# Two transformer layers on one core: the four compute engines' instruction orders laid out anew

## The chip, the core and the metric

The kernel runs on one core of one Trainium2 chip. Its time is the device time of one execution in microseconds (us); less is better. A core has four compute engines that each work through an instruction list of their own in the order in which it was written: TensorE (PE in the profile), VectorE (DVE), ScalarE (ACT) and GpSimd (POOL). SyncE (SP) issues nearly all DMAs here, also in written order. Engines wait for each other through semaphores only. An instruction that waits holds up everything that is behind it on its engine.

## The reference

Input is one sequence of 2048 tokens with 128 features. Four blocks follow, each `x = x + block(layernorm(x))`:

```python
x = x + L0_attn(layernorm(x))   # 16 heads of 64: softmax over the own segment of 64 and over
                                # positions at distance 4, 8, ..., 256; then w_o
x = x + L0_ffn(layernorm(x))    # blockwise FP4 quantised gate, up and down products, silu
x = x + L1_attn(layernorm(x))   # RMS norms, gated linear recurrence in chunks of 64, an MLP of 512
x = x + L1_ffn(layernorm(x))    # token shift, sigmoid gate, squared relu
```

The first block is the attention, with projections q, k and v of 1024 columns. The other three work token by token, but for the recurrence and the token shift.

## The kernel before, in words

The attention is cut into 32 units, numbered 0 to 31: 8 pairs of heads times 4 windows of 512 tokens. Unit U has pair U // 4 and window U % 4. Each unit passes through these steps, which are small functions in the code, called with the unit and often with a part:

- on PE: `project(U, 1)` and `project(U, 0)` make keys and queries (lines 403 to 405), `scores(U, 0)` and `scores(U, 1)` the two halves of the scores (line 422), `turn(U, 0..3)` transposes four parts of the weights (line 464), `weigh(U, 0..3)` multiplies them by the values (lines 484, 495, 498), and `output(U)` by w_o (line 510). For the values themselves there are 32 calls `values(i)` (lines 388 to 390), all before the loop.
- on DVE: `seg_max` (lines 731, 733), `band_max` (line 719), `seg_sums` (741), `differences` (750, 754), `factors` (761 to 771), `even_turned` (780), which copies the transposed parts 0 and 2 out of PSUM, `accumulate` (792), and `take_values` of odd index (836).
- on ACT: `take_keys`, `take_queries` (601, 609), `band_exps`, `seg_exps` (569, 577), `exp_difference` (616), `odd_turned` (585) for parts 1 and 3, `take_out` (593), and `take_values` of even index (644).
- on POOL: `keys_by_class`, `queries_by_class` (930, 938), `scale_band`, `scale_seg` (948, 957).

The softmax has two halves, which lie differently over the partitions. Each unit therefore sends its maxima and sums to DRAM and reads them back in the other layout: `send_statistics` (lines 306, 307) and `fetch_statistics` (314, 315) on SP. `differences` of the unit waits for the landing of that. `factors` and the scaling on POOL follow, and the turns wait for the scaling.

A list written out by hand sets the order of units 0 to 3 with all `values`; SP stores each of these values (line 268) between the exchanges. Then a loop `for t in range(6, 33)` has one iteration on each engine for a step. In iteration t PE projects unit t, makes the scores of unit t-2 and turns and weighs units t-5 and t-6. After the loop a second list finishes the attention and interleaves it with the token blocks of layers 0 and 1. These go in four groups of 512 tokens (g = 0 to 3), with steps such as `t1`, `x1`, `bn0`, `qx0`, `z0`, `rs0` (lines 1100 and on). Group g begins with `t1(g)`, which needs `accumulate(28 + g)`.

PSUM has eight banks. Scores take banks 0 to 3. Banks 4 and 5 hold the turned parts, even parts in 4 and odd in 5, and before the loop the values of even and odd index. Each of the two holds one such part at a time, so a turn waits for the copy of the part before. `weigh` fills bank 6. Bank 7 is shared by keys, output and queries in turn; the list `occupants` says in which order. Statistics, `pband` and `pseg` have four slots, rows of keys and queries three.

Of the kernel before, what the change touches and what calls it, by code (L numbers as in the profile page):

```python
# [22 lines left out]
P = 128  # L23
# [85 lines left out]
def attention(nc, ctx, hidden, w_q, w_k, w_v, w_o, w_gate, w_up, w_down, plain_weights, columns, ident, constants,  # L109
# [121 lines left out]
    occupants = [(0, "key")]  # L231
    for x in range(1, FIRST_STEP):
        occupants += [(x, "key"), (x - 1, "query")]
    occupants.append((FIRST_STEP - 1, "query"))
    for t in range(FIRST_STEP, NS_ALL + 8):
        occupants += [(t - lag, who) for who, lag in (("key", 0), ("wo", 7), ("query", 0)) if there(t - lag)]
# [21 lines left out]
    with nc.Block() as block:  # L258
# [106 lines left out]
        def _(pe):  # L365
# [148 lines left out]
            keep_busy(7); turn_rows(0); keep_busy(4)  # L514
            values(0); values(1); values(2); project(0, 1); turn_rows(1); values(3); project(1, 1); values(4)
            values(5); turn_rows(2); values(6); project(0, 0); values(7); values(8); project(2, 1); values(9)
            values(10); turn_rows(3); scores(0, 0); scores(0, 1); values(11); values(12); project(1, 0); values(13)
            values(14); project(3, 1); values(15); scores(1, 0); scores(1, 1); project(2, 0); values(16); values(17)
            project(4, 1); values(18); values(19); scores(2, 0); scores(2, 1); values(20); values(21); project(3, 0)
            values(22); values(23); values(24); project(5, 1); values(25); values(26); scores(3, 0); values(27)  # L520
            values(28); project(4, 0); values(29); values(30); project(5, 0); values(31); turn(0, 0); scores(3, 1)
            turn(0, 1); turn(0, 2)

            for t in range(FIRST_STEP, DRAIN):
                project(t, 1)
                weigh(t - 6, 0)
                weigh(t - 6, 1)
                turn(t - 6, 3)  # L530
                output(t - 7)
                turn(t - 5, 0)
                weigh(t - 6, 2)
                scores(t - 2, 0)
                weigh(t - 6, 3)
                scores(t - 2, 1)
                project(t, 0)
                turn(t - 5, 1)
                turn(t - 5, 2)
# [3 lines left out]
            output(26); turn(27, 3); weigh(27, 0); weigh(27, 1); weigh(27, 2); scores(31, 0); weigh(27, 3)  # L543
            scores(31, 1); turn(28, 0); turn(28, 1); output(27); turn(28, 2); turn(28, 3); weigh(28, 0); weigh(28, 1)
            weigh(28, 2); weigh(28, 3); turn_weights(0); turn_weights(1); turn(29, 0); output(28); turn_weights(2)
            turn(29, 2); turn(29, 1); t1(0); turn_weights(3); turn_weights(4); turn(29, 3); turn_weights(5)
            weigh(29, 0); weigh(29, 1); weigh(29, 2); weigh(29, 3); turn_weights(6); turn(30, 0); turn(30, 1)
            output(29); turn_weights(7); turn(30, 3); turn(30, 2); weigh(30, 0); weigh(30, 1); t1(1); weigh(30, 2)
            weigh(30, 3); turn(31, 1); t2(0); turn(31, 0); turn(31, 3); output(30); turn(31, 2); gu0(0); t1(2)
            weigh(31, 0); weigh(31, 1); weigh(31, 2); weigh(31, 3); gu1(0); output(31); t2(1); t1(3); gu2(0); gu0(1)  # L550
            gu3(0); gu1(1); t2(2); gu2(1); gu0(2); gu1(2); t2(3); gu3(1); gu0(3); gu2(2); t3a(0); gu1(3); t3b(0)
            gu3(2); dn(0); gu2(3); t3a(1); t3b(1); gu3(3); dn(1); t4(0); pv(0); pk(0); t3a(2); pg(0); t3b(2); pa(0)
            pq(0); t4(1); dn(2); qq(0); pv(1); t3a(3); pk(1); t3b(3); pg(1); dn(3); pa(1); t4(2); pq(1); trx(0)
            qq(1); pv(2); pk(2); pg(2); t4(3); op(0); pv(3); trx(1); pq(2); pk(3); pa(2); pg(3); pa(3); op(1); qq(2)
            pq(3); t5(0); qq(3); trx(2); fc1(0); fc0(0); trx(3); fc3(0); t5(1); fc2(0); fc0(1); fc1(1); op(2); pr(0)
            fc2(1); fc3(1); op(3); t5(2); pr(1); fc0(2); fc1(2); t5(3); fc2(2); fc3(2); fc1(3); fc0(3); t6(0); fc3(3)
            pr(2); t6(1); fc2(3); k(0); pr(3); r(0); t6(2); k(1); k(2); kv(0); t6(3); r(1); kv(1); r(2); k(3); kv(2)
            r(3); kv(3)

        @block.scalar  # L560
        def _(act):
# [93 lines left out]
            split_v(0); deviations(0); split_qk(0, 1); take_hi(0); split_qk(0, 0); take_values(0); deviations(1)  # L655
            take_keys(0); take_hi(1); take_values(2); deviations(2); take_keys(1); take_values(4); take_hi(2)
            deviations(3); take_values(6); split_v(1); take_queries(0); take_values(8); take_keys(2); take_values(10)
            take_hi(3); band_exps(0, 0); take_values(12); take_queries(1); take_values(14); take_keys(3); seg_exps(0)
            band_exps(0, 1); take_queries(2); take_values(16); seg_exps(1); band_exps(1, 0); take_values(18)
            take_keys(4); band_exps(1, 1); take_values(20); seg_exps(2); take_values(22); take_queries(3)  # L660
            take_values(24); band_exps(2, 0); exp_difference(0); take_keys(5); take_values(26); band_exps(2, 1)
            take_values(28); take_queries(4); take_values(30); band_exps(3, 0); exp_difference(1); take_queries(5)
            odd_turned(0, 1); take_keys(6); seg_exps(3); odd_turned(0, 3); band_exps(3, 1)
            for t in range(FIRST_STEP, DRAIN):
                exp_difference(t - 4)
                take_out(t - 6)
                take_queries(t)
                odd_turned(t - 5, 1)
                take_keys(t + 1)
                band_exps(t - 2, 0)  # L670
                odd_turned(t - 5, 3)
                seg_exps(t - 2)
                band_exps(t - 2, 1)
                if t in (6, 7):
                    split_qk(1, 7 - t)
                if t in (QUANT_STEP + 2, QUANT_STEP + 7, QUANT_STEP + 12):
                    coarse_weights((t - QUANT_STEP) // 5)

# [3 lines left out]
            exp_difference(29); take_out(27); band_exps(31, 0); odd_turned(28, 1); odd_turned(28, 3); seg_exps(31)  # L682
            band_exps(31, 1); take_out(28); exp_difference(30); take_weights(0); take_weights(1); take_weights(2)
            odd_turned(29, 1); take_weights(3); odd_turned(29, 3); take_weights(4); z0(0); take_out(29)
            exp_difference(31); odd_turned(30, 1); take_weights(5); take_weights(6); take_weights(7); qx6(0)
# [12 lines left out]
        def _(dve):  # L698
# [139 lines left out]
            def blocks(x):  # L838
                return x.rearrange("p (b x) -> p b x", x=QB)
# [82 lines left out]
        def _(pool):  # L922
# [74 lines left out]
            for t in range(FIRST_STEP, DRAIN):  # L997
# [5 lines left out]
                if t == 8:  # L1003
                    tail_constants(pool, constants, s_made, s_cols)
# [983 lines left out]
```

## Time and profile before

| | us |
|---|---|
| three runs | 470.03, 474.9, 470.95 |
| median | 470.95 |
| span of the profiled execution, first to last instruction | 468.2 |
| PE busy | 443.3 (95%) |
| DVE busy | 394.1 (84%) |
| ACT busy | 333.0 (71%) |
| POOL busy | 296.5 (63%) |

The profiled execution has no total time beside its span. The fastest of the three runs is 1.8 us over that span, the median 2.75 us. A matmul's end is modelled in the profile, and matmuls overlap, so a PE that is called busy in all of a stretch has had no gap of its own there; it says nothing on how much work was in it.

### The profile page before, as it was taken

The numbers are of one execution on the slowest core, as the hardware profiler recorded it, in microseconds if no ns is written. First come the engines' busy times: TensorE is split into PE (matmuls) and PEld (weight loads), VectorE is DVE, ScalarE is ACT, GpSimd is POOL, SyncE is SP. The second block draws the span as 40 slices with busy tenths as digits, with TensorE's granted clock in tenths as the row PEclk, the third lists the DMA queues.
The fourth block names the chain that finished last, engine by engine and source line by source line (L and its number), as shares of the span: only waits on it lengthen the run. The fifth ranks groups of instructions, "written<-read, shape, count | busy, mean of one in ns | idle before, by whom it ended". The sixth has DMA issues, their size and how long they took to land.

```text
span 468.2 us, 17264 instructions
## 1 busy us (share of the span) xinstructions
PE 443.3 (95%) x6440; PEld 348.8 (74%) x6440; DVE 394.1 (84%) x1344; ACT 333.0 (71%) x975; POOL 296.5 (63%) x491
## 2 busy tenths in 40 slices
PE   7999699999999999999999899998987989999996
PEld 5687588888888888888787678887744757558775
DVE  5888598997988899799797697996899989998775
ACT  3678668778768777877786678695566579987533
POOL 4222576687576768667865587665669897674322
PEclk9999999999999999999999999999999999999999
DMA  6477952356345335445455564464000000000003
GB/s 224 175 254 201 276 122 53 75 115 123 75 84 110 74 74 109 81 78 109 86 116 122 110 135 90 77 123 91 1 1 0 0 2 0 2 0 2 1 0 91
DMA packets 136098, 40.53 MB, mean 87 GB/s; under 512 B 104976, under 2 KB 131024, under 8 KB 136016
## 3 DMA queue, kind: packets, MB, share of 16 engines
q1 hardware_dynamic: 135440, 38.38, 35.9%
q8 instruction: 52, 0.85, 0.8%
q10 hardware_dynamic: 576, 1.05, 0.6%
q14 instruction: 30, 0.25, 0.2%
HBM read 29.44 MB, written 9.96 MB: 84 GB/s over the span
## 4 chain that ended last, share of the span: by engine, by line
PE 59%; POOL 9%; DMA 8%; DVE 8%; ACT 7%; SPq 4%; issue 3%; ACTq 0%; POOLq 0%; DVEq 0%
PE psum L464 10%; PE psum L422 10%; PE psum L484 5%; PE psum L1186 5%; PE psum L498 5%; PE psum L495 4%; PE psum L510 4%; PE psum L403 4%; DMA st<-w_rows_dram 3%; DMA w_rows_dram<-st 3%; PE psum L1181 3%; ACT pband L569 3%; PE psum L405 2%; PE psum L404 2%; POOL area L1827 2%
## 5 line engine op out<-in xcount | busy, mean ns | idle before, releaser
L948 POOL TENSOR_SCALAR pband<-pband,fac 128x192 f32<-128x192 f32 x256 | 103.9, 424 | 84.8 <-DVE fac L771 84.7
L569 ACT ACTIVATE pband<-pband,st 128x192 f32<-128x192 f32 x256 | 113.2, 448 | 0.9 <-DVE st L719 0.9
L719 DVE CUSTOM_DVE_ANT_0 pband<-psum,band_mask 128x192 f32<-128x192 f32 x256 | 76.0, 353 | 0.1
L422 PE MATMUL psum<-keys,q_class 64*64 64x192 f32 (+2 forms) x1536 | 66.3, 274 | 0.0
L464 PEld LDWEIGHTS psum<-ident,pband 128*128 128x128 f32 x384 | 45.3, 141 | 25.5 <-issue 17.8
L464 PE MATMUL psum<-ident,pband 128*128 128x128 f32 x384 | 53.1, 273 | 6.1 <-DVE arena L836 3.1
L422 PEld LDWEIGHTS psum<-keys,q_class 64*64 64x64 f32 x1536 | 57.7, 133 | 1.4 <-issue 1.4
L569 ACT ACTIVATION_READ_ACCUMULATOR pband<-pband,st 128x1 f32 x256 | 49.5, 193 | 0.0
L938 POOL COPY q_class<-q_rows 128x512 f32<-128x512 f32 x32 | 36.4, 1137 | 14.0 <-ACT q_rows L609 14.0
L930 POOL COPY keys<-k_rows 128x512 f32<-128x512 f32 x32 | 36.2, 1131 | 14.3 <-issue 7.2
L780 DVE COPY pt<-psum 128x512 f32<-128x512 f32 x64 | 43.6, 682 | 0.4
L585 ACT COPY pt<-psum 128x512 f32<-128x512 f32 x64 | 37.2, 581 | 4.9 <-PE psum L464 4.9
L741 DVE TENSOR_REDUCE st<-pseg 128x8 f32<-128x512 f32 x32 | 21.9, 685 | 19.9 <-ACT pseg L577 19.9
L609 ACT COPY q_rows<-psum 128x512 f32<-128x512 f32 x32 | 18.8, 587 | 27.6 <-PE psum L405 27.6
L498 PE MATMUL psum<-pt,v_seg 64*64 64x64 f32 x1024 | 35.6, 218 | 0.5 <-issue 0.5
L1181 PE MATMUL psum<-xt,arena 128*128 128x512 f32 x72 | 35.1, 603 | 0.8 <-ACT xt L1422 0.8
L957 POOL TENSOR_TENSOR pseg<-pseg,fac 128x512 f32<-128x512 f32 x32 | 33.8, 1056 | 2.9 <-DVE fac L771 2.9
L484 PEld LDWEIGHTS psum<-pt,v_both 128*64 128x64 f32 x512 | 27.3, 136 | 10.5 <-issue 10.5
L484 PE MATMUL psum<-pt,v_both 128*64 128x128 f32 x512 | 35.0, 279 | 0.0
L498 PEld LDWEIGHTS psum<-pt,v_seg 64*64 64x64 f32 x1024 | 32.8, 135 | 0.7 <-issue 0.7
L510 PE MATMUL psum<-o_sb,wo 128*128 128x512 f32 x64 | 33.0, 597 | 0.1
L422 PE MATMUL psum<-k_rows,q_rows 64*64 64x64 f32 x1024 | 32.0, 223 | 0.0
(213 smaller groups left out, 1086.4 us busy)
## 6 DMA issues: line engine op xcount, KB each, us to landing
v_rows_dram<-arena SPq DMA_DIRECT2D x32, 256.0 KB, 4.6
v_both<-v_rows_dram SPq DMA_DIRECT2D x32, 256.0 KB, 3.9
v_seg<-v_rows_dram SPq DMA_DIRECT2D x64, 128.0 KB, 3.8
v_side<-v_rows_dram SPq DMA_DIRECT2D x96, 64.0 KB, 2.6
w_rows_dram<-st SPq DMA_DIRECT2D x64, 8.0 KB, 3.0
st<-w_rows_dram SPq DMA_DIRECT2D x64, 8.0 KB, 2.5
arena<-_attn_hidden_states_dram SPq DMA_DIRECT2D x4, 256.0 KB, 3.9
out_dram<-x SPq DMA_DIRECT2D x4, 256.0 KB, 2.5
```

The costliest lines, as they stand in the source:

```text
L422: return pe.matmul(bank[2 * r + head][rows, at:at + y.shape[1]], x, y, start=True, stop=True, skip_group_check=True)
L464: last = pe.transpose(turn_bank[odd][:, P * k:P * (k + 1)], src, ident[:, :])
L484: last = pe.matmul(by_class[dims, c, :], v_both[:, c, w, dims], turned[:, P * k:P * (k + 1)], start=(b == 0 and k < 2), stop=False, skip_g ...
L498: last = pe.matmul(out_bank[dims, cols], v_seg[dims, 2 * (TW * w + k) + half, :], turned[dims, cols], start=False, stop=(k == 3 and half = ...
L510: pe.matmul(shared_bank[:, :], wo[:, U // NW, :], o_sb[:, :], start=True, stop=True).then_inc(s_mix, 1)
L569: act.activation(x, x, ACT.Exp, bias=mine[:, head:head + 1], scale=-1.0, accum_out=mine[:, 2 + head:3 + head]).then_inc(s_exp, 1)
L585: act.copy(pt[:, PT_SLOTS + e % PT_SLOTS, :], turn_bank[1][:, :]).then_inc(s_pt[1], 1)
L719: dve.tensor_tensor_reduce(pband[:, G % P_SLOTS, c, head, :], bank[2 * r + head][:, at:at + BAND], band_mask[:, (0, 1, 1, 2)[w], SEG * (1 ...
L780: dve.tensor_copy(pt[:, e % PT_SLOTS, :], turn_bank[0][:, :]).then_inc(s_pt[0], 1)
L938: pool.tensor_copy(q_class[:, G % ROW_SLOTS, :, :], q_rows[:, G % ROW_SLOTS, :].rearrange("p (x c) -> p c x", c=DIL)).then_inc(s_qclass, 1)
L948: pool.tensor_scalar(x, x, fac[:, F % 2, 1, c, head:head + 1], 1.0, ALU.mult, ALU.mult).then_inc(s_scaled, 1)
L1181: end(pe.matmul(bk(g, to)[:, :], w, x, start=True, stop=True, skip_group_check=True), g, "tensor")
```

## The change

Every engine's list and loop are written in another order. No operation is added or taken away, none moves to another engine, and SP's list stays as it is. In the loop POOL's iteration is shifted: it now begins with `queries_by_class(t - 5)` and ends with both halves of `scale_band(t - 8)`. The list `occupants` is written out to match, with the same order for the loop's units. A few lines of the STEPS table are only wrapped differently.

```diff
+            def zero_pads():        # the two memsets that stood in the loop at t == 8
...
 PE
             for t in range(FIRST_STEP, DRAIN):
+                turn(t - 6, 1)
+                turn(t - 6, 2)
                 project(t, 1)
                 weigh(t - 6, 0)
                 weigh(t - 6, 1)
                 turn(t - 6, 3)
                 output(t - 7)
-                turn(t - 5, 0)
+                scores(t - 2, 0)
                 weigh(t - 6, 2)
-                scores(t - 2, 0)
                 weigh(t - 6, 3)
                 scores(t - 2, 1)
+                turn(t - 5, 0)
                 project(t, 0)
-                turn(t - 5, 1)
-                turn(t - 5, 2)
...
 ACT
             for t in range(FIRST_STEP, DRAIN):
+                take_out(t - 6)
                 exp_difference(t - 4)
-                take_out(t - 6)
                 take_queries(t)
                 odd_turned(t - 5, 1)
                 take_keys(t + 1)
                 band_exps(t - 2, 0)
-                odd_turned(t - 5, 3)
                 seg_exps(t - 2)
+                odd_turned(t - 5, 3)
                 band_exps(t - 2, 1)
...
 DVE
             for t in range(FIRST_STEP, DRAIN):
+                accumulate(t - 7)
+                seg_sums(t - 3)
+                seg_max(t - 2, 0)
+                band_max(t - 2, 0)
                 differences(t - 4)
                 even_turned(t - 5, 0)
-                factors(t - 4)
-                band_max(t - 2, 0)
-                seg_max(t - 2, 0)
-                even_turned(t - 5, 2)
                 seg_max(t - 2, 1)
+                factors(t - 4)
+                even_turned(t - 5, 2)
                 band_max(t - 2, 1)
-                seg_sums(t - 2)
-                accumulate(t - 6)
...
 POOL
             for t in range(FIRST_STEP, DRAIN):
-                scale_band(t - 5, 1)
-                keys_by_class(t)
-                scale_seg(t - 5)
-                scale_band(t - 4, 0)
-                queries_by_class(t - 1)
+                queries_by_class(t - 5)
+                scale_seg(t - 9)
+                keys_by_class(t - 3)
+                scale_band(t - 8, 0)
+                scale_band(t - 8, 1)
```

ACT's extra work in some iterations (`split_qk`, `coarse_weights`) now stands before `take_keys` and no longer at the iteration's end.

**PE in the loop**, one step from the projections of keys on. Line 464 (465 after) is `turn`, 510 (511) `output`, 495 and 498 (496, 499) `weigh` 2 and 3, 422 (423) `scores`, 403 (404) the first product of `project`. Before:

```order
L464 MATMUL psum<-ident,pseg 128x128 x4
L510 MATMUL psum<-o_sb,wo 128x512
L464 MATMUL psum<-ident,pband 128x128 x4
L495 MATMUL psum<-pt,v_side 64x64 x8
L422 MATMUL psum<-keys,q_class 64x192 x2
...
L498 MATMUL psum<-pt,v_seg 64x64 x16
...
L403 MATMUL psum<-xn_hi,w_hi 128x512
L404 MATMUL psum<-xn_lo,w_hi 128x512
L405 MATMUL psum<-xn_hi,w_lo 128x512
L464 MATMUL psum<-ident,pband 128x128 x8
```

Now:

```order
L465 MATMUL psum<-ident,pseg 128x128 x4
L511 MATMUL psum<-o_sb,wo 128x512
L423 MATMUL psum<-keys,q_class 64x192 x2
...
L496 MATMUL psum<-pt,v_side 64x64 x8
L499 MATMUL psum<-pt,v_seg 64x64 x16
...
L465 MATMUL psum<-ident,pband 128x128 x4
L404 MATMUL psum<-xn_hi,w_hi 128x512
L405 MATMUL psum<-xn_lo,w_hi 128x512
L406 MATMUL psum<-xn_hi,w_lo 128x512
L465 MATMUL psum<-ident,pband 128x128 x8
```

`turn(·, 0)`, four transposes, went from behind `output` to just ahead of the queries' projection. The eight transposes behind that are `turn(·, 1)` and `turn(·, 2)`.

**DVE before the loop**, around `differences(0)` (lines 750, 754 before, 747, 751 after). Line 836 (833) is `take_values`, 741 (738) `seg_sums`, 719 (716) `band_max`, 761 to 771 (758 to 768) `factors`. Before:

```order
L836 COPY arena<-psum 128x512
L741 TENSOR_REDUCE st<-pseg 128x4x2
L836 COPY arena<-psum 128x512
L719 ISA pband,st<-psum,band_mask 128x192
...
L750 TENSOR_REDUCE joint<-st 128x16
L754 TENSOR_TENSOR diff<-joint,st 128x32
L836 COPY arena<-psum 128x512
L761 TENSOR_TENSOR part<-ediff,st 128x32
```

Now:

```order
L833 COPY arena<-psum 128x512
L747 TENSOR_REDUCE joint<-st 128x16
L751 TENSOR_TENSOR diff<-joint,st 128x32
L833 COPY arena<-psum 128x512
L716 ISA pband,st<-psum,band_mask 128x192
...
L833 COPY arena<-psum 128x512 x2
L758 TENSOR_TENSOR part<-ediff,st 128x32
```

`take_values(23)`, both halves of `band_max(2)` and `seg_sums(2)` stood ahead of `differences(0)` and stand behind it now. In the same list `differences(1)` went from ahead of `take_values(31)` to behind it.

**DVE after the loop**, around `differences(30)`. Line 780 (777) is `even_turned`, 792 (789) `accumulate`, 1526 (1527) `x1(0)`. Before:

```order
L741 TENSOR_REDUCE st<-pseg 128x4x2
L750 TENSOR_REDUCE joint<-st 128x16
L754 TENSOR_TENSOR diff<-joint,st 128x32
L1520 MEMSET mark 128x512
L1521 MEMSET zt 128x1
L780 COPY pt<-psum 128x512
L792 TENSOR_TENSOR arena<-psum,arena 128x512
```

Now:

```order
L738 TENSOR_REDUCE st<-pseg 128x4x2
L777 COPY pt<-psum 128x512
L747 TENSOR_REDUCE joint<-st 128x16
L751 TENSOR_TENSOR diff<-joint,st 128x32
L789 TENSOR_TENSOR arena<-psum,arena 128x512
L758 TENSOR_TENSOR part<-ediff,st 128x32
```

`even_turned(29, 0)` now stands ahead of `differences(30)`. On ACT `band_exps(31, 1)` went the other way, from ahead of `exp_difference(30)` to behind it.

## Rows read from the trace of the kernel before

**Rows 1.** Windows: stretch; busy us of each engine; clock, DMA share, GB/s
```profile
60.00:248.00 188.00, 188.00 (x3685) 156.02 (x3685) 164.97 (x649) 145.75 (x480) 134.39 (x239) 1.00 0.46 93
248.00:270.00 22.00, 19.84 (x375) 15.87 (x376) 14.94 (x63) 13.92 (x48) 13.00 (x24) 1.00 0.54 115
270.00:338.00 68.00, 66.30 (x1189) 54.78 (x1187) 57.93 (x215) 49.35 (x157) 46.36 (x87) 1.00 0.43 86
338.00:418.00 80.00, 71.32 (x410) 47.19 (x410) 74.04 (x160) 61.10 (x128) 64.68 (x82) 1.00 0.00 1
418.00:468.20 50.20, 46.02 (x284) 34.87 (x284) 37.67 (x95) 24.71 (x62) 15.44 (x19) 0.98 0.07 22
```

**Rows 2.** Chain that ended last, 188 to 204 us: start, us, what
```profile
192.46 0.43 PE psum L403
...
193.36 0.87 PE psum L464 x8
194.23 0.30 PE psum L403
...
195.00 1.02 PE psum L484 x16
196.02 0.59 PE psum L464 x4
...
197.47 0.44 PE psum L464 x4
```

**Rows 3.** Timeline of DVE, one step: start, us, instruction [idle before <-releaser]
```profile
198.41 0.69 DVE L741 TENSOR_REDUCE st<-pseg 128x8 f32<-128x512 f32 x1 [0.53 <-ACT pseg L577]
...
199.96 0.68 DVE L780 COPY pt<-psum 128x512 f32<-128x512 f32 x1
```

**Rows 4.** Groups of instructions by line, DVE: busy us, mean ns | idle before
```profile
L719 DVE CUSTOM_DVE_ANT_0 pband<-psum,band_mask 128x192 f32<-128x192 f32 x256 | 76.0, 353 | 0.1
...
L733 DVE TENSOR_TENSOR pseg<-st,psum 128x256 f32<-128x256 f32 x64 | 26.9, 421 | 2.2
```

**Rows 5.** Timeline of DVE before the loop and at its second step
```profile
47.31 0.20 DVE L750 TENSOR_REDUCE joint<-st 128x16 f32<-128x32 f32 x1 [1.75 <-DMA st<-w_rows_dram]
...
57.06 0.19 DVE L750 TENSOR_REDUCE joint<-st 128x16 f32<-128x32 f32 x1 [4.71 <-DMA st<-w_rows_dram]
...
73.93 0.19 DVE L750 TENSOR_REDUCE joint<-st 128x16 f32<-128x32 f32 x1 [1.12 <-DMA st<-w_rows_dram]
```

**Rows 6.** Timeline of PE before the loop
```profile
45.16 0.39 PE L388 MATMUL psum<-w_hi,xn_hi 128*128 128x512 f32 x1
...
58.23 1.23 PE L464 MATMUL psum<-ident,pband 128*128 128x128 f32 x8 [3.06 <-DVE arena L836]
```

**Rows 7.** Timeline of SP before the loop and in its first steps
```profile
43.16 0.46 SPq L314 DMA_DIRECT2D st<-w_rows_dram  x1
...
51.54 0.81 SPq L314 DMA_DIRECT2D st<-w_rows_dram  x1
...
70.66 0.33 SPq L314 DMA_DIRECT2D st<-w_rows_dram  x1
```

**Rows 8.** Timeline of DVE, where transfers for the tail are added
```profile
267.21 0.19 DVE L750 TENSOR_REDUCE joint<-st 128x16 f32<-128x32 f32 x1 [3.83 <-DMA st<-w_rows_dram]
```

**Rows 9.** Timeline of DVE after the loop
```profile
317.48 0.20 DVE L750 TENSOR_REDUCE joint<-st 128x16 f32<-128x32 f32 x1 [1.86 <-DMA st<-w_rows_dram]
...
324.54 0.19 DVE L750 TENSOR_REDUCE joint<-st 128x16 f32<-128x32 f32 x1 [1.22 <-DMA st<-w_rows_dram]
```

**Rows 10.** Timeline of PE after the loop
```profile
319.20 1.06 PE L464 MATMUL psum<-ident,pband 128*128 128x128 f32 x8 [1.39 <-DVE pt L780]
```

**Rows 11.** Timeline of SP after the loop
```profile
317.41 0.54 SPq L306 DMA_DIRECT2D w_rows_dram<-st  x1
```

**Rows 12.** Timeline of POOL, 319 to 337 us
```profile
323.28 1.04 POOL L1877 TENSOR_TENSOR rs<-rs,minus_half 128x4 f32<-128x4 f32 x1
```

**Rows 13.** Chain that ended last, from 400 us
```profile
411.17 2.09 POOL rs L1877
```

More of the change, by code:

```diff
@@ L544, in _ @@
[L544 to L558, printed above, removed]
+            turn(27, 1); output(26); turn(27, 3); turn(27, 2); weigh(27, 0); weigh(27, 1); scores(31, 0); weigh(27, 2)
@@ L659, in _ @@
[L659 to L662, printed above, removed]
+            split_v(0); deviations(0); take_hi(0); split_qk(0, 1); split_qk(0, 0); split_v(1); take_values(0)
@@ L681, in _ @@
              sr) = tail_scalar(act)
[L682 to L685, printed above, removed]
-            odd_turned(30, 3); take_out(30); odd_turned(31, 1); odd_turned(31, 3); z0(1); silu0(0); qx6(1)
@@ L872, in _ @@
[L872 to L876 removed]
+            moments(0); normalise(0); split_v(0); take_lo(0); moments(1); split_qk(0, 1); split_qk(0, 0); normalise(1)
@@ new lines, in _ @@
+            moments(2); take_values(1); take_lo(1); take_values(3); normalise(2); take_values(5); moments(3)
+            take_lo(2); take_values(7); normalise(3); take_values(9); take_lo(3); take_values(11); split_v(1)
+            band_max(0, 0); seg_max(0, 0); take_values(13); seg_max(0, 1); band_max(0, 1); seg_sums(0)
+            take_values(15); band_max(1, 0); seg_max(1, 0); take_values(17); band_max(1, 1); seg_max(1, 1)
+            take_values(19); seg_max(2, 0); seg_sums(1); seg_max(2, 1); take_values(21); differences(0)
@@ L877, in _ @@
+            take_values(23); band_max(2, 0); band_max(2, 1); take_values(25); take_values(27); factors(0); seg_sums(2)
+            take_values(29); band_max(3, 0); take_values(31); even_turned(0, 0); seg_max(3, 0); differences(1)
+            even_turned(0, 2); factors(1); seg_max(3, 1); band_max(3, 1)
             for t in range(FIRST_STEP, DRAIN):
+                accumulate(t - 7)
+                seg_sums(t - 3)
+                seg_max(t - 2, 0)
+                band_max(t - 2, 0)
                 differences(t - 4)
-                even_turned(t - 5, 0)
@@ L901, in _ @@
              xr, k1, k2, o0, o) = tail_vector(dve)
-            differences(29); band_max(31, 0); factors(29); even_turned(28, 0); seg_max(31, 0); seg_max(31, 1)
-            even_turned(28, 2); band_max(31, 1); accumulate(27); seg_sums(31); differences(30); clear()
-            even_turned(29, 0); accumulate(28); factors(30); x1(0); bn0(0); ag0(0); even_turned(29, 2)
-            differences(31); qx0(0); qx1(0); qx2(0); even_turned(30, 0); factors(31); accumulate(29)
-            even_turned(30, 2); qx7(0); qx8(0); x1(1); xq(0); bn0(1); ag0(1); even_turned(31, 0); xqt(0)
```

178 lines of the change are left out of this document (100 added, 78 removed), and 16 rows, old and new, of the table STEPS.

## The prediction

> **What bounds the kernel now.** I read the windows first, since nothing changes but orders: what an order can give is idle time of the engine that sets the pace, and nothing else. From 60 to 248 us PE is busy 188.00 of 188.00 us, DVE 165 [rows 1]. The chain of waits confirms it: in this stretch it stays on PE from product to product and never steps to another engine; a piece of it is in [rows 2]. A loop step is pure PE work of about 8.8 us, or 9.3 where `weigh(·, 2)` is whole. Orders cannot shorten that; they can only lengthen it by a wait. From 248 to 270 PE lacks 2.2 us, from 270 to 338 1.7 us. From 338 to 418 no engine is full: PE lacks 8.7 us, DVE 6.0. From 418 on the chain is on PE again, 46.0 busy of 50.2 [rows 1], and the rest is the last results' way out.
>
> So what lies open is: the stretch before 60 us, whose largest hole is 3.06 us before PE's first turns in the loop's order [rows 6]; 2.2 us at 250 to 270; 1.7 us up to 338; and at most DVE's 6.0 us in 338 to 418. In all about 13 us, 2.8% of 468.2, if an order found all of it.
>
> **The loop.** The junctions of PE first. In the step, PE goes between 128-row and 64-row products. Four transposes take 0.59 us behind a 64-row product and 0.44 behind a 128-row one, a projection's first product 0.43 behind scores and 0.30 behind transposes [rows 2]. Before: output, turn 0 (0.44), weigh, scores, weigh, scores, projection (0.43): 0.87. Now: output, scores, weigh, weigh, scores, turn 0 (0.59), projection (0.30): 0.89. Over 27 iterations that is 0.02 x 27 = 0.5 us. The entry into the 64-row products comes once in either order. The Trainium skill (TensorEngine Tiling (Array Packing), Key Properties) says that a change of tiling mode drains TensorE; it would charge per switch, and counting switches alone, as many before as now, it gives 0 where the rows give 0.5.
>
> Then a new wait. `turn(·, 2)` needs bank 4, so it needs the copy `even_turned(·, 0)` of `turn(·, 0)`. Before, a weigh, both scores, a weigh, the projection and `turn(·, 1)` lay between, over 4 us. Now it is only the projection and `turn(·, 1)`: 0.77 (194.23 to 195.00) + 0.44 (half of 0.87) = 1.2 us [rows 2]. The copy takes 0.68 [rows 3], and 0.14 passes from a copy's end to a waiting turn's start in the tail (318.37 + 0.69 is 319.06, PE starts at 319.20 [rows 10]). That leaves 0.3 us, or 0.1 when I count that a PE restarted after a wait is slower into its first product. It holds only if DVE is free when `turn(·, 0)` ends. From the end of `scores(·, 0)` DVE has seg_max (a reduce and a subtraction, 0.42 each), band_max (four of 353 ns that overlap, 1.1) and differences (0.19 twice): 2.3 us [rows 4, 5]. PE in that time has two weighs, the other scores and the turn, about 3.0 us in a short step and 3.5 in a long one. DVE may thus be 0.7 us late. What makes it late is `seg_sums`, which now heads the step and waits for `seg_exps`, as it waits 0.53 us before [rows 3]; by following ACT's list through (take_keys, band_exps, seg_exps) I find it 0.2 to 0.3 late. **I take 0 for this wait**; its bounds are 0 and what the rival below says.
>
> The exchange of statistics: `band_exps(·, 1)` still ends the same time after the keys' projection, and `differences` still must start at about the start of the queries' projection for the turns to be in time (then by way of `even_turned(·, 2)`'s turn, now too). So the allowance for the round trip stays, and so does the loss at 267 us, where differences come 3.83 us late by the profile [rows 8] and PE loses 2.2 us. One thing is worse there: `coarse_weights(2)`, 0.5 us of ACT, now stands ahead of `band_exps(22, ·)`, and the serial chain of SP behind it starts that much later: **+0.5**.
>
> **Before the loop.** The gain is plain: `turn(0, 1)` waited for `take_values(31)`, which stood behind `differences(1)`, which waited 4.71 us for its landing at 57.06 [rows 5, 6]. With `take_values(31)` ahead the 3.06 us are gone: -3.1. Against it stands `differences(0)`. It lands at 47.31 behind a fetch at 43.16 [rows 5, 7], and nothing brings that forward, since SP issues DMA after DMA from 28 us on in an unchanged list. DVE waited 1.75 us for it with `band_max(2, 1)` done. Now `take_values(23)` (0.6), `band_max(2)` (2 x 1.1) and `seg_sums(2)` (0.6) are behind the wait, 3.4 us more of it. PE needs `take_values(23)` for `values(25)`, which started at 45.16 [rows 6], with the same products ahead of it now. It will start at 47.31 + 0.4 + 0.6 = 48.3: a wait of about 3 us. From 47.3 on, DVE has all its work up to `even_turned(0, 0)`, 9.7 us, and arrives at 57. Following the four lists from there, I get `weigh(1, 0)` about 0.9 us earlier than before. But then `differences(3)` is awaited: the fetch was at 70.66, the landing at 73.93 [rows 5, 7]. The fetch of unit 1, at 51.54 [rows 7], now needs `take_values(25)` and (26), which come near 52.0, so SP's list runs 0.5 us late, and at t = 7 `split_qk` (0.6) stands between differences and the copy that the new wait needs. That gives the 0.9 back. **Sum before the loop: 0**, between -3.1 (all kept) and +3 (the new wait, nothing regained).
>
> **After the loop.** `even_turned(29, 0)` waited behind `differences(30)`, which landed at 317.48, and PE stood for 1.39 us [rows 9, 10]. That goes. In return `band_exps(31, 1)` is behind `exp_difference(30)` and ends near 320.0 (317.48, differences 0.4, the exp 0.2, four exps of 0.44). Unit 31's statistics, sent at 317.41 before and landed at 324.54 [rows 9, 11], are sent at 320 and land at 327.1, the same 7.1 us later. That costs nothing by itself: ACT came to `exp_difference(31)` late before, behind `z0(0)`, and DVE now has `qx0` to `qx2` of group 0 ahead of `differences(31)`. DVE's idle of 1.86 and 1.22 us and what it waited for `z0(0)` (4.4 in all) become some 2.8 us, and group 1 comes 1.5 us earlier to its first quantising. From there DVE is nearly full, so the lead lasts: **-1.5 us**. The order of the other steps to 418 differs by swaps of neighbours. Such swaps turn waits by tenths; I put them at **-0.5**, between -3 (half of DVE's 6.0 us) and +2. The end from 418 is PE work in all but the same order: 0.
>
> **Sum.** +0.5 +0.5 +0 -1.5 -0.5 = -1.0 us. The span goes from 468.2 to 467.2. The median of the runs stands 2.75 us above the span, so 469.9; I write 469.8.
>
> **The rivals.**
> 1. *All is kept.* The 3.1 us before the loop survive because statistics land sooner than I think, and the tail finds half of DVE's idle: -3.1 -1.5 -3.0 + 1.0 = -6.6, so 470.95 - 6.6 = 464.4; with only one of the two it is 466 to 467. I write 465.5. For: the holes are real [rows 6, 10]. Against: SP's own pace. Chance 0.20.
> 2. *The short way from turn 0 to turn 2 (slower).* If DVE comes more than 0.3 us late to `even_turned(·, 0)`, PE waits in every step. It decides from the point where DVE has less than 2.3 us between the end of `scores(·, 0)` and that of `turn(·, 0)`. At 0.3 us in each of 27 steps it costs 8 us: 478 us; where only the 15 steps with a piece of `quantise` are late, 4.5 us: 474. For: the margin is 0.1 to 0.3 us, and no row of before shows such a wait. Against: DVE idles over 1 us in each step. Chance 0.17.
> 3. *The wait before `values(25)` is not regained.* +3.0 -1.0 = +2.0: 473. Against: DVE had 4.71 us to spare right behind it. Chance 0.13.
> 4. *GpSimd slows in the tail.* One and the same small op of POOL takes 1.04 us at 323 and 2.09 at 411 [rows 12, 13], and new neighbours on DVE may make more of them slow; with three in the chain that is +3 us, 473. Chance 0.05. The Trainium skill (SBUF — State Buffer, Who interferes with whom) says that GpSimd and a VectorE instruction with two SBUF inputs hold one port in turn; by that rule the two rows differ by what VectorE ran, as DVE was nearly full at 411.
>
> My forecast has the remaining 0.45.
>
> **Range and chances.** Three runs of the kernel before lie 1% apart at most, and under 1% (4.7 us) I call it no change. Faster by over 1% needs 466.2 or less: most of rival 1 and a little of the forecast, 0.19. Slower by over 1% needs 475.7: most of rival 2 and a bit of 3 and 4, 0.16. Within 1%: 0.65. The range is 464.5 to 476.0: it takes in rival 1, rivals 3 and 4, and rival 2 where only part of the steps wait.
>
> **What would show it.** Steps right: the chain of waits stays on PE from 60 to 248 us, with 8.8 and 9.3 us from one first `weigh` to the next. DVE waits 4 us and more before 47.3, PE about 2.8 us before the 26th `values`, and no 3 us before the first turns. PE's 1.39 us before the turns near 319 are gone. Wrong: turns (line 465) released by a DVE copy in each step; `differences(0)` landing near 44; the first step over 1 us earlier than before; DVE with less than 4 us of idle in 338 to 418. The prediction fails most easily in the tail, where I followed the lists to 345 us only, and by the margin of turn 2.

## The result

The changed kernel takes 482.41 us (median of 4 runs, 481.82 to 484.08) beside 471.78 us of the kernel before on the same chip (median of 4): ratio 1.0225, 95% interval 1.0178 to 1.0272. It is about 2.2% slower, and the forecast of 469.8 us (464.5 to 476.0) missed it. The profiled execution took 482.27 us; its span is 480.4 us, 12.2 more than before.

Its windows, cut so that the work in them answers to [rows 1] (columns as there):
```profile
60.00:248.00 188.00, 180.78 (x3516) 146.05 (x3512) 172.72 (x623) 138.20 (x458) 128.84 (x220) 1.00 0.44 89
248.00:278.00 30.00, 29.40 (x558) 23.83 (x558) 27.44 (x105) 22.28 (x75) 20.18 (x34) 1.00 0.58 127
278.00:346.00 68.00, 66.05 (x1168) 52.81 (x1166) 58.28 (x204) 47.96 (x152) 44.86 (x88) 1.00 0.43 83
346.00:428.00 82.00, 72.06 (x413) 47.70 (x412) 77.53 (x159) 60.39 (x126) 64.48 (x82) 1.00 0.00 1
```
PE, full from 60 to 248 us before, now lacks 7.2 us there, with fewer products in it (3516 for 3685), and DVE is busy 7.8 us more with less work done. The clock is the same. Page and groups by line, of after:
```profile
PE 448.0 (93%) x6440; PEld 345.9 (72%) x6440; DVE 418.5 (87%) x1344; ACT 331.5 (69%) x975; POOL 297.0 (62%) x491
...
PE 45%; DVE 24%; issue 9%; POOL 6%; SPq 6%; DMA 6%; ACT 2%; DVEq 0%; POOLq 0%; ACTq 0%
...
L751 DVE TENSOR_TENSOR diff<-joint,st 128x32 f32<-128x32 f32 x32 | 26.7, 835 | 1.1
```
DVE's 1344 instructions are the same as before and take 24 us more. 17.0 of it is one group of 32: the subtraction in `differences`, 302 ns on average before and 835 now. Another 3.9 are in the last product of `factors` (32 of them, 175 ns each before, up to 0.95 us now). The chain of waits that ended last is on PE for 45% of the span (59% before) and on DVE for 24% (8%).

What holds the subtraction can be seen in one step. DVE, then GpSimd, then PE (start, us, instruction):
```profile
216.68 0.19 DVE L747 TENSOR_REDUCE joint<-st 128x16 f32<-128x32 f32 x1
216.90 1.33 DVE L751 TENSOR_TENSOR diff<-joint,st 128x32 f32<-128x32 f32 x1
218.15 0.68 DVE L777 COPY pt<-psum 128x512 f32<-128x512 f32 x1
```
```profile
211.74 1.14 POOL L929 COPY keys<-k_rows 128x512 f32<-128x512 f32 x1 [2.82 <-ACT k_rows L598]
212.88 3.21 POOL L947 TENSOR_SCALAR pband<-pband,fac 128x192 f32<-128x192 f32 x8
216.04 1.13 POOL L937 COPY q_class<-q_rows 128x512 f32<-128x512 f32 x1
217.13 1.05 POOL L956 TENSOR_TENSOR pseg<-pseg,fac 128x512 f32<-128x512 f32 x1
220.99 1.14 POOL L929 COPY keys<-k_rows 128x512 f32<-128x512 f32 x1 [2.81 <-ACT k_rows L598]
```
```profile
218.98 0.63 PE L465 MATMUL psum<-ident,pband 128*128 128x128 f32 x4 [0.36 <-DVE pt L777]
...
220.23 1.10 PE L485 MATMUL psum<-pt,v_both 128*64 128x128 f32 x16
229.65 1.09 PE L485 MATMUL psum<-pt,v_both 128*64 128x128 f32 x16
238.90 1.09 PE L485 MATMUL psum<-pt,v_both 128*64 128x128 f32 x16
248.16 1.09 PE L485 MATMUL psum<-pt,v_both 128*64 128x128 f32 x16
```
GpSimd works without a gap from `keys_by_class` at 211.74 to the end of `scale_seg` at 218.18 (217.13 + 1.05). DVE's subtraction, 0.19 us where it is alone, begins at 216.90 and ends at 218.23, 0.05 after GpSimd. It is not the only one: 25 of the 32 subtractions took 0.5 us or more, and each of them ended 0.04 to 0.06 us behind the end of a run of GpSimd. Behind the subtraction in DVE's list stands `even_turned(17, 0)`, the copy for which `turn(17, 2)` waits. This closes a ring: ACT's copy of the keys releases GpSimd's run, the run's end releases the subtraction, then come DVE's copy, PE's turn, the projection of the next keys and ACT's next copy of keys. It goes round in 9.25 us (211.74 to 220.99). The steps of PE from unit 17 to 21 take 9.42, 9.25, 9.26 and 9.39 us where they took 9.26, 9.26, 8.79 and 8.79: the long steps hardly lose, the short ones are stretched to the ring. From 76 to 258 us PE waits 4.7 us for DVE's copy, in 11 of its turns.

I read the losses off the first `weigh` of a unit (x16 of PE line 485, 484 before), by how much later it starts than the same one before: unit 2 at 80.18 for 77.30 (+2.9), unit 21 at 257.55 for 248.62 (+8.9), unit 31 at 346.13 for 337.89 (+8.2), and the end of the span +12.2. Entry, loop and end each have a share. The loop's is steady: in three more traces with the same order up to there (experiments 3, 4 and 5) units 2 to 21 lose 6.0 to 6.4 us, here 6.1. The entry's is not: unit 2 stands at +1.0, +1.6 and +2.2 there, and in four traces with the entry of before at -1.1 to +0.7.

### The profile page after: what moved, and what is told of

It reads as the page before. It is cut to its first block, busy times and chain, and to the rows that moved or that the text cites. A ratio compares the mean times of both kernels' runs of the same rounds, so it can differ in the third digit from the quotient of the medians.

```text
span 480.4 us, 17264 instructions
## 1 busy us (share of the span) xinstructions
PE 448.0 (93%) x6440; PEld 345.9 (72%) x6440; DVE 418.5 (87%) x1344; ACT 331.5 (69%) x975; POOL 297.0 (62%) x491
## 3 DMA queue, kind: packets, MB, share of 16 engines
q10 hardware_dynamic: 576, 1.05, 0.7%
## 4 chain that ended last, share of the span: by engine, by line
PE 45%; DVE 24%; issue 9%; POOL 6%; SPq 6%; DMA 6%; ACT 2%; DVEq 0%; POOLq 0%; ACTq 0%
PE psum L465 8%; PE psum L423 5%; PE psum L1187 5%; PE psum L485 5%; PE psum L511 4%; DVE pband L716 3%; SPq L293 3%; DVE pt L777 2%; PE psum L499 2%; PE psum L496 2%; DMA w_rows_dram<-st 2%; PE psum L1182 2%; DMA st<-w_rows_dram 2%; PE psum L404 2%; PE psum L406 2%
## 5 line engine op out<-in xcount | busy, mean ns | idle before, releaser
L423 PEld LDWEIGHTS psum<-keys,q_class 64*64 64x64 f32 x1536 | 52.9, 133 | 22.2 <-issue 22.2
L465 PE MATMUL psum<-ident,pband 128*128 128x128 f32 x384 | 57.9, 279 | 6.7 <-DVE pt L777 6.5
L423 PE MATMUL psum<-keys,q_class 64*64 64x192 f32 (+2 forms) x1536 | 61.6, 276 | 0.0
L465 PEld LDWEIGHTS psum<-ident,pband 128*128 128x128 f32 x384 | 42.8, 140 | 16.6 <-issue 10.1
L937 POOL COPY q_class<-q_rows 128x512 f32<-128x512 f32 x32 | 36.3, 1133 | 11.7 <-ACT q_rows L606 11.7
L613 ACT ACTIVATE ediff<-diff 128x32 f32<-128x32 f32 x32 | 7.3, 230 | 40.5 <-DVE diff L751 40.5
L598 ACT COPY k_rows<-psum 128x512 f32<-128x512 f32 x32 | 18.8, 586 | 22.2 <-PE psum L406 22.1
L956 POOL TENSOR_TENSOR pseg<-pseg,fac 128x512 f32<-128x512 f32 x32 | 33.4, 1043 | 0.0
L404 PE MATMUL psum<-xn_hi,w_hi 128*128 128x512 f32 x64 | 29.7, 464 | 0.0
```

Source lines behind the costliest of these rows:

```text
L404: pe.matmul(shared_bank[:, :], hi, xn_hi[:, cols], start=True, stop=False)
L423: return pe.matmul(bank[2 * r + head][rows, at:at + y.shape[1]], x, y, start=True, stop=True, skip_group_check=True)
L465: last = pe.transpose(turn_bank[odd][:, P * k:P * (k + 1)], src, ident[:, :])
```

## The experiments

Each kernel ran beside the kernel before; R is its ratio to that, with the 95% interval. The changed kernel has R 1.0225. It ran beside a median of 471.78 us, all others beside 467.9 to 469.6, so differences of a few tenths of a percent between it and them say nothing.

**1. Is it the ring?** On DVE the copy goes ahead of the subtraction:
```diff
-                differences(t - 4)
                 even_turned(t - 5, 0)
+                differences(t - 4)
```


> The changed kernel with one swap on DVE in the loop: even_turned(t-5, 0) stands ahead of differences(t-4). Theory P (GpSimd holds DVE's subtraction on two SBUF operands until its own run of back-to-back work ends, and that subtraction stands on the way from turn 0 to turn 2): the subtraction keeps its about 0.8 us, but PE no longer waits for it; the short steps come back to 8.8 us, the loop gets back 5 to 7 us of its 7.7, so 475 to 478. Theory L (the subtraction is long because it waits for the landing of the statistics, so the exchange sets the pace): the swap gives nothing, since exp_difference and factors come even later, 482 to 484. Theory B (what was lost lies before the loop and behind it, the loop being as before): 482, within 1.

It took 485.94 us, R 1.0359 (1.0315 to 1.0403): a miss, slower still. Yet the subtraction fell to 226 ns on average, less than forecast. PE now waits one product later:
```profile
219.79 0.50 PE L404 MATMUL psum<-xn_hi,w_hi 128*128 128x512 f32 x1 [0.27 <-ACT q_rows L606]
```
ACT has `exp_difference`, which needs `differences`, ahead of `take_queries`, and the projection needs that copy. So a second way back to PE ran through `differences`. In the next kernel both are opened (on ACT `take_queries(t)` goes ahead of `exp_difference(t - 4)` as well):

> The changed kernel with two swaps in the loop: on DVE even_turned(t-5, 0) ahead of differences(t-4), and on ACT take_queries(t) ahead of exp_difference(t-4). With the first swap alone ACT's take_queries stood behind the exponential of differences, and PE's next projection waited for it. Theory P (two short ways between PE's turn 0 and its next work run through differences, held or not): with both copies ahead nothing between them depends on differences, steps come back to 8.8 and 9.26 us, and since differences then starts as GpSimd's run ends, its subtraction stays at 0.25 us. The loop gets back 6 to 8 us: ratio to the kernel before 1.003 to 1.010 instead of 1.0225 of the changed kernel. Theory Q (GpSimd's run or ACT's own list paces the loop in the new order): ratio 1.02 and more.

474.67 us, R 1.0106 (1.007 to 1.0142), a hair above the forecast of theory P. The subtraction takes 217 ns, and from unit 2 to 21 the first `weigh` loses nothing (+2.97 to +2.79): the loop's loss is gone by two swaps. ACT's swap alone was not run. That the ring also runs through GpSimd's run and through the held subtraction is what experiments 2 and 3 show.

**2. GpSimd's phase.** GpSimd's order of before in the changed kernel, GpSimd's changed order in the kernel before, and the changed kernel with the scaling of bands cut short (`x = pband[..., 0:8]` in `scale_band`):

> The changed kernel with GpSimd's orders before and in the loop as in the kernel before; everything else as changed. Theory P: differences(.) takes about 0.42 us again where it falls in GpSimd's idle time, DVE's busy time falls from 418.5 to about 395 to 400, the short steps come back to 8.8 us: 473 to 477. If the new place of differences on DVE still meets a run of GpSimd, it stays long in part: then 478 to 481 and DVE busy 405 to 412. Theory L: 482. Theory B: 482.

> The kernel before with the changed kernel's orders of GpSimd before and in the loop alone. Theory P: differences heads DVE's step here and its copy of turn 0 has 4 us until turn 2 needs it, so even a held subtraction costs PE nothing: 470 to 473; whether the subtraction grows shows where GpSimd's run now lies. If GpSimd's order alone were the loss (scaling comes too late for turns 1 and 2): 478 to 482.

> The changed kernel with GpSimd's scaling of the bands cut to the first 8 columns of each (the rest stays unscaled, so this computes less): the four instructions of each scale_band stay, their semaphores too, but GpSimd's run behind keys_by_class gets over 2 us shorter and no longer reaches differences. Nothing of DVE, ACT or PE is changed. Theory P: differences falls to about 0.42 us, DVE's busy time to 395 to 400, short steps to 8.8 us: 473 to 476. Theory L: no change of DVE's subtraction, 481 to 483. Theory B: 481 to 483.

The first took 498.68 us, R 1.0638 (1.0595 to 1.0681): the time is a miss, while DVE's work shrank as forecast (subtraction 272 ns, DVE busy 399.2). PE's scores now wait for the classes of the queries. The second took 499.14 us, R 1.0648 (1.0594 to 1.0701), a miss too. A row of each:
```profile
220.87 0.90 PE L423 MATMUL psum<-keys,q_class 64*64 64x192 f32 x24 [0.83 <-POOL q_class L937]
```
```profile
L754 DVE TENSOR_TENSOR diff<-joint,st x32: 191/2299/2365, 48.0 to 357.2; 128x32 f32<-128x32 f32 x32
```
The second row gives least, median and most ns: in the old order of DVE, with GpSimd's new one, the subtraction is held for 2.3 us in most steps (193 ns is its median in before). GpSimd's order and those of the others are one piece; changing one alone costs 20 to 30 us. The third took 475.92 us, R 1.0157 (1.0098 to 1.0217), as forecast by theory P: subtraction 201 ns, and units 2 to 21 lose 0.5 us instead of 6.1 (+1.2 to +1.7), though DVE, ACT and PE have the changed kernel's lists.

**3. What is held?** The subtraction replaced by another instruction on the same 128x32 elements in the same place:
```diff
-                dve.tensor_tensor(diff, joint (broadcast), tops, ALU.subtract)
+                dve.tensor_scalar(diff, tops, 0.0, 1.0, ALU.mult, ALU.mult)      # first
+                dve.reciprocal(diff, st[..., 2:4])                               # second
```


> The changed kernel, all orders as changed, with the subtraction in differences replaced by a tensor_scalar on the statistics alone (times 0, times 1; so the factors are not the reference's): the same 128x32 elements, the same waits, the same place, but one operand in SBUF instead of two. Theory P (an instruction of DVE that reads two SBUF operands is held while GpSimd works through its run, one that reads a single operand is not): its mean falls from 835 ns to 190 to 260, none over 0.4 us, the loop's short steps come back to 8.8 us, DVE's busy time to 395 to 402, ratio 1.008 to 1.014. Theory L (the instruction at this place is long whatever it reads, for a semaphore or a landing): mean stays near 800 ns, ratio 1.020 to 1.026.

> The changed kernel, all orders as changed, with the subtraction in differences replaced by a reciprocal of the statistics' sums (so the factors are not the reference's): the same 128x32 elements, waits and place. With a tensor_scalar on one operand the instruction still took 913 ns on average and the time was 1.0214, while the reduction just ahead of it and the RECIPROCAL in factors never grew (190 and 253 ns in every run). Theory P2 (not the number of operands but the kind of the instruction decides: TENSOR_TENSOR on two SBUF operands and TENSOR_SCALAR are held by GpSimd's run, TENSOR_REDUCE and RECIPROCAL are not): 300 to 500 ns at every one of the 32 places, DVE's busy time 400 to 408, the loop's short steps at 8.8 to 8.9 us, the first weigh of unit 21 at +1 to +4 against before instead of +7 to +9, ratio 1.010 to 1.017. Theory L (whatever stands at this place is long, for a semaphore): a mean of over 700 ns and 1.020 to 1.026.

With `tensor_scalar` it took 480.27 us, R 1.0214 (1.0184 to 1.0244), the instruction 913 ns on average: both as theory L had it, and my theory P in its form "two SBUF operands" fell. With `reciprocal` it took 476.3 us, R 1.0143 (1.0089 to 1.0196), as theory P2 had it, and theory L fell: the waits and the place are the same. Least, median and most ns of the instruction; after (with DVE's subtraction in `seg_max`, which reads one operand in PSUM), then the two kernels:
```profile
L751 DVE TENSOR_TENSOR diff<-joint,st x32: 191/711/1364, 47.6 to 335.1; 128x32 f32<-128x32 f32 x32
...
L730 DVE TENSOR_TENSOR pseg<-st,psum x64: 420/422/423, 29.6 to 319.5; 128x256 f32<-128x256 f32 x64
```
```profile
L751 DVE TENSOR_SCALAR diff<-st x32: 181/1131/1766, 47.5 to 333.8; 128x32 f32<-128x32 f32 x32
```
```profile
L751 DVE RECIPROCAL diff<-st x32: 352/353/355, 47.5 to 327.1; 128x32 f32<-128x32 f32 x32
```
Held are the TENSOR_TENSOR with both inputs in SBUF and the TENSOR_SCALAR from SBUF to SBUF. The RECIPROCAL never is, nor the TENSOR_TENSOR with an input in PSUM, nor the TENSOR_REDUCE just ahead (187 to 195 ns). The RECIPROCAL had its chance to be: 28 of its 32 lie in a run of GpSimd. With it unit 21 stands at +1.9 instead of +8.9. The Trainium skill (SBUF — State Buffer, Who interferes with whom) says that VectorE shares a port pair with GpSimd, and that a copy or `tensor_scalar` in a 2-port mode needs the pair, a TENSOR_TENSOR with two SBUF inputs its read side, a TENSOR_REDUCE never. The rows agree. It says that one holder keeps the pair for its instruction; here the hold outlasted one: that at 216.90 began in GpSimd's L937 copy, which ended at 217.17, and went on through all of L956.

**4. Loop or end?** Here the kernel before runs up to the end of the loop and then has the changed kernel's end; then the reverse:

> The kernel before up to the end of the loop, with the changed kernel's orders behind the loop on all four engines (without what the loop of before has done already). Theory S (the loss is in two places that add up, loop and end): the loop as before, PE's stall near 319 us gone (-1.0 to -1.5 us), then +4 to +6 us from the swaps at 370 and 420: ratio 1.006 to 1.012. Theory T (the end loses only because the loop hands over late and out of phase): 0.996 to 1.000, by the end's own forecast of -2 us.

> The changed kernel up to the end of the loop, with the orders of before behind it. Theory S: +7 to +8 us of the loop and nothing else: ratio 1.014 to 1.018. Theory T: as theory S or better, since part of the delay is absorbed at the end by what PE waited for there.

R 1.0123 (1.0073 to 1.0172; 475.01 us) and 1.0139 (1.0108 to 1.0169; 476.19 us). Within the intervals the two add up to the changed kernel's loss: theory S. With the old end the delay of +5.8 at unit 31 stays +5.8 to PE's last product; with the new one PE's last product is 3.4 us later than unit 31's `weigh` alone would make it, in the changed kernel as here.

**5. The end.** In the kernel of experiment 4 with the new end PE waits near 371 us:
```profile
371.37 1.06 PE L1235 MATMUL psum<-ident,area 128*128 128x128 f32 x8 [2.02 <-POOL area L1833]
374.83 0.86 PE L1214 MATMUL psum<-grid,xt 128*128 128x352 f32 x2 [0.77 <-DVE area L1589]
...
```
Two first tries: in the changed kernel one neighbour was put back on PE (`gu2(3)` ahead of `t3a(1)`), and in the kernel before all engines but DVE were given the new end:

> The changed kernel with one swap of neighbours undone on PE behind the loop: gu2(3) ahead of t3a(1) again, as before. Theory S: PE waits up to 3 us for GpSimd's quantising ahead of t3a(1) and t3b(1), and gu2(3), whose silu2(3) and hm2(3) sit in DVE's and ACT's full lists, now waits with it; undoing it gives back 2 to 3 us: ratio 1.016 to 1.019. Theory U (DVE's and GpSimd's own order decides there): 1.021 to 1.024.

> The kernel before with the changed kernel's orders behind the loop on PE, ACT and GpSimd, but DVE's as before. With DVE's changed too it was 1.0123. Theory V (DVE's own order behind the loop costs: hm1(3) behind qb0(2), and qa7, qa8 beside GpSimd's scaling): 1.000 to 1.005. Theory U2 (the order of PE and ACT costs: gu2(3) and silu2(3) behind the transposes that wait for GpSimd): 1.008 to 1.012.

The first took 481.75 us, R 1.0263 (1.0226 to 1.0299): nothing gained. `gu2(3)` then waited 1.68 us for DVE's `hm1(3)` instead, which stands behind `qb0(2)` now. The second took 484.17 us, R 1.0339 (1.0271 to 1.0408), far outside both expectations; like experiment 2 it shows only that lists must match. So, in the kernel with the new end, the piece around `gu2(3)` was put back on PE, ACT and DVE, then a second piece on DVE (`s(2); m(2)` ahead of `aa(3); e1(3)`, and `x3_(2)` ahead of `x23(0)`):

> The kernel before with the changed kernel's end on all engines (1.0123), and in it the piece around PE's gu2(3) put back as before on three engines: PE gu2(3) ahead of t3a(1), ACT silu2(3) ahead of ht0(1), DVE qa7(1) ahead of qa2(2) and hm1(3) ahead of qb0(2). On PE alone, this swap had given nothing, since gu2(3) then waited for DVE's hm1(3). If the loss at 370 us is this knot of three lists: 2 us back by dn(1), of which 1 to 2 are left at the end, 1.008 to 1.010. If it is GpSimd's slowed quantising: nothing, 1.012.

> The kernel before with the changed kernel's end, and in it two pieces put back: the one around gu2(3) as in the run before, and DVE's s(2), m(2) ahead of aa(3), e1(3) with x3_(2) ahead of x23(0). GpSimd's y(2), which PE's op(2) waits for, stands behind m(2), and came 0.9 us later and took 2.1 us instead of 1.4. If these two pieces are the loss of the end: by the trace op(2) 1.5 to 2 us earlier against the first piece alone, span at or under that of before, ratio 0.998 to 1.006. If other swaps take it over: 1.008 to 1.012.

473.53 us, R 1.0118 (1.0075 to 1.0161), and 473.01 us, R 1.0067 (1.0032 to 1.0103). From unit 31's `weigh` to PE's last product the traces lose 3.4 us with the new end, 2.4 with one piece back and 1.6 with both. The times do not resolve either piece: the three intervals overlap (R 1.0123, 1.0118, 1.0067). What remains is more than those 1.6 us: with both pieces back the new end still has R 1.0067, and in experiment 7 it costs 4 us (471.19 for 467.2) beside the old end on the same chip. It lies in swaps I didn't single out.

**6. The entry.** In the trace with the two swaps of experiment 1, 3.7 us were still lost between unit 1 and unit 2:
```profile
70.89 1.12 PE L511 MATMUL psum<-o_sb,wo 128*128 128x512 f32 x2 [1.85 <-DMA wo<-in_L_attn_w_o_dram]
```
`accumulate(0)`, which heads DVE's step now, waited with `output(0)`. On top of the two swaps, `load_wo()` was put ahead of `load_sides(0, 3)` in SP's list:

> The changed kernel with the two swaps in the loop (the copy of turn 0 ahead of differences on DVE, take_queries ahead of exp_difference on ACT), and in SP's list load_wo() ahead of load_sides(0, 3). With the two swaps alone, the first weigh of unit 2 came 3.7 us later against before than that of unit 1: output(0) waited 1.9 us for the load of wo, and accumulate(0), which heads DVE's next step, waited with it. Theory W (the load of wo, pushed back by SP's list, is the loss at the loop's entry): the first weigh of unit 2 comes 2.5 to 3.7 us earlier, the loop ends 1.5 to 3 us earlier, ratio 1.003 to 1.008. Theory X (the exchange of statistics sets the entry, and the load only hides it): ratio 1.009 to 1.012, and differences(3) or (4) awaited instead.

474.12 us, R 1.0118 (1.0078 to 1.0158), where theory W had 1.003 to 1.008: a miss. The time is no better than 1.0106; in the trace the wait is gone and unit 2 stands at -0.4 instead of +3.0. Not every execution has this wait: with the same entry the load was issued at 64.7 to 66.1 us instead of 67.66 in three other traces, and PE waited for it in none of them. What the load costs in the mean stays open.

**7. The gains I had counted on, and the sum.** The kernel before with DVE's two swaps alone (`take_values(31)` ahead of `differences(1)`; `even_turned(29, 0)` ahead of `differences(30)`):

> The kernel before with two swaps on DVE alone, those from which the prediction took its gains: take_values(31) ahead of differences(1) before the loop, and even_turned(29, 0) ahead of differences(30) behind it. If both holes (3.06 us before the first turns, 1.39 us near 319 us) are real gains that the rest of the change buried: ratio 0.991 to 0.994, 3 to 4 us. If the exchange of statistics takes the first back at differences(3) and the group work takes the second: 0.997 to 1.002.

468.65 us, R 1.002 (0.9987 to 1.0053). This is what the second expectation said. By its trace unit 0 is 2.5 us earlier and unit 2 1.0; near 319 us 1.4 are gained and kept. The first gain is not shown even by the trace: experiment 4's kernel with the entry of before stands at -1.7 and -1.1 there. The second is less than runs of one kernel differ. Then all causes at once, in the changed kernel with the old end and with the new:

> The changed kernel up to the end of the loop with three swaps (copy of turn 0 ahead of differences, take_queries ahead of exp_difference, load_wo ahead of load_sides(0, 3)), and the orders of before behind the loop. If loop, entry and end are all of the loss: ratio 0.996 to 1.004. If something of it is still unnamed: 1.006 and more.

> The changed kernel with the three swaps up to the loop and both pieces of the end put back, all else as changed: six places out of some hundreds. If these are the causes: ratio 0.998 to 1.006. If the rest of the orders costs too: 1.008 and more.

With the old end **467.2 us, R 0.9946 (0.9925 to 0.9966): half a percent faster than the kernel before, and better than forecast**. With the new end and two pieces back 471.19 us, R 1.0021 (1.0001 to 1.0041). Windows of the first, for [rows 1]:
```profile
60.00:248.00 188.00, 188.00 (x3690) 154.28 (x3690) 169.65 (x657) 144.05 (x482) 135.78 (x231) 1.00 0.47 96
248.00:270.00 22.00, 21.63 (x412) 17.32 (x413) 18.44 (x74) 16.70 (x57) 15.29 (x27) 1.00 0.54 111
```
PE is full again, and has lost 0.4 us at 248 to 270 where before it lost 2.2: a gain of the new order that its losses had buried. It is smaller than these two rows say, since five other traces with the loop of before lose 0.4 to 1.7 there, and three others with the mended loop 0 to 0.4. The hold is not gone but moved. GpSimd now holds the last product of `factors`, for which PE doesn't wait (mean of 413 ns for 175 in the kernel before):
```profile
L769 DVE TENSOR_TENSOR fac<-ediff,inverse x32: 174/175/1107, 53.9 to 326.5; 128x16 f32<-128x16 f32 x32
```
One more swap on top:

> The kernel of the three swaps with the old end, which took 0.9946 of before, and in its end even_turned(29, 0) ahead of differences(30) on DVE. In the kernel before the same swap brought PE 1.4 us forward near 319 us by the trace, to the end of the span. If it adds here: 0.990 to 0.993. If the lead that this kernel has there already holds it: 0.993 to 0.996.

467.53 us, R 0.9945 (0.9921 to 0.9968): nothing more, as the second expectation said.

## Why the prediction was wrong

- **The wait of turn 2, taken as 0: the step that failed.** The wait was seen and the margin (0.1 to 0.3 us) as well; rival 2 had its mechanism, 8 us and 478. What failed is the size of a term in it: `differences` was counted as 0.19 twice [rows 5]. The subtraction took 0.84 on average and 1.33 where it mattered. PE waited for the copy behind it for 4.7 us in the loop, and units 2 to 21 lost 6.1. I costed each instruction by its row of before and never asked what GpSimd would be doing at its new place. The effect stood in the trace of before, in a subtraction with a median of 193 ns and a mean of 302, and I had its rule in rival 4, for the end alone. That rival 2's 8 us lay near the loop's 6.1 is in part luck: it had DVE late by its own work, not held by GpSimd.
- **PE's junctions, +0.5.** In the mended kernel steps of 8.75 stand for 8.79: they cost nothing, if anything they give 0.04 a step.
- **`coarse_weights` at 267, +0.5.** Wrong in sign. `differences(23)`, which waited 3.83 us [rows 8], waits 0.66 now, and 2.4 us of the loop's delay are absorbed from unit 21 to 23. The mended kernel gains 2.1 us there against the one trace of before, but five other traces with the loop of before gain 0.5 to 1.8 on it as well.
- **Before the loop, 0.** The landing came as said: 47.35 for 47.31, and the turns' 3.06 us [rows 6] are gone. `values(25)` waited 1.30 us where 3 were forecast. But unit 2 is 2.9 late in this trace (1.0 to 2.2 in three others). Rows of after (DVE, then PE, then SP):
```profile
47.35 0.19 DVE L747 TENSOR_REDUCE joint<-st 128x16 f32<-128x32 f32 x1 [2.58 <-DMA st<-w_rows_dram]
...
66.84 0.19 DVE L747 TENSOR_REDUCE joint<-st 128x16 f32<-128x32 f32 x1 [1.66 <-DMA st<-w_rows_dram]
```
```profile
48.52 0.47 PE L389 MATMUL psum<-w_hi,xn_hi 128*128 128x512 f32 x1 [1.30 <-DVE arena L833]
...
68.01 0.63 PE L465 MATMUL psum<-ident,pband 128*128 128x128 f32 x4 [1.47 <-DVE pt L777]
72.37 1.13 PE L511 MATMUL psum<-o_sb,wo 128*128 128x512 f32 x2 [1.41 <-DMA wo<-in_L_attn_w_o_dram]
```
```profile
67.66 0.60 SPq L299 DMA_DIRECT2D wo<-in_L_attn_w_o_dram  x1
```
  I had SP 0.5 us late and followed that only to statistics. `differences(2)` landed late for the copy behind it, and the load of `wo`, last of the loads in the same queue, was issued 3.5 us later than the 64.15 of before.
- **After the loop, -1.5.** The stall of 1.39 [rows 10] is gone, and DVE's swap alone earns 1.4 in the trace. In the changed kernel nothing of it is left: +7.1 at unit 27 has become +8.2 at unit 31, ahead of which PE waits 0.71 us for GpSimd's `scale_seg` and 0.33 for ACT.
- **Swaps of neighbours, -0.5, bounds -3 and +2.** They cost 3.4 us from unit 31's first `weigh` to PE's last product (+8.2 to +11.6), beyond my bound. DVE has only 4.5 us idle of the 82 from 346 to 428. That a transpose which waits 2 us for GpSimd ahead of `gu2(3)` delays what DVE and ACT have in line is argued from the rows; putting the piece back did not show in the times.
- **Rival 4.** The small op of 2.09 us [rows 13] takes 0.98 to 0.99 in after's chain and 1.58 at most, and GpSimd's busy time is 297.0 us for 296.5: not the cause. GpSimd was to be slowed by DVE; it was DVE that GpSimd slowed, and in the loop.

## What to carry to other kernels

When an order moves an instruction of DVE that GpSimd can hold, cost it by the end of GpSimd's run of back-to-back work at its new place, not by its duration at the old one; least, median and most ns of its line show whether it was held before. Where a forecast hangs on a margin of tenths, find every way by which the producer's result comes back to PE: here there were two. Orders of several engines fit as a whole, so mend them by single swaps and don't carry over one engine's list.

## What was not expected of the hardware

The text ahead of the prediction says that engines wait for each other through semaphores only. Here DVE waited inside an instruction. One of 0.19 us took up to 2.37 us; in most cases it was held past the end of single GpSimd instructions, to 0.05 us behind the last of an unbroken run. Not always: in the kernel with GpSimd's changed order alone (experiment 2) the subtraction at 64.63 came through in 0.34 us, between two of GpSimd's scalings, in a run that went on to 68.59. What decides between the two stays open. GpSimd's run held a TENSOR_SCALAR with one SBUF input as well (up to 1.77 us) and never a RECIPROCAL of the same elements (352 to 355 ns).
